# One pass over two attention blocks and a feed-forward block: earlier stack loads, a reordered slot plan, masked maxima in one instruction, a shared last tile, and a query norm applied as a factor

## What is computed

```python
# causal attention, 16 heads of 16, the whole 2048 x 2048 triangle
dot = jnp.einsum('bqhd,bkhd->bhqk', q, k)
dot = jnp.where(causal[None, None], dot, -jnp.inf)
attn = jax.nn.softmax(dot, axis=-1)
out = jnp.einsum('bhqk,bkhd->bqhd', attn, v)
...
# one layer of the fourth block: windows of 128 tokens, 8 heads of 64, then the gated feed-forward
q = l2norm(q) * qs
k = l2norm(k) * ksc
q, k = rotary_xpos(q, k)
o = local_attention(q, k, v)          # each window sees itself and the one before
x = x + o @ wo
h = (h - mu) / jnp.sqrt(var + 1e-05) * lg + lb
h = h @ w1 + b1                       # w1 is 256 x 1364
a, g = jnp.split(h, 2, axis=-1)       # 682 columns each
h = a * jax.nn.gelu(g, approximate=False)
x = x + h @ w2 + b2
```

## Time and profile before

| | us |
|---|---|
| three runs, median (lowest to highest) | 4441.09 (4441.04 to 4442.19) |
| the profiled execution, its own time | 4444.75 |
| its span, first to last instruction | 4443.1 |
| PE busy | 3852.1 (87%) |
| DVE busy | 2924.3 (66%) |
| ACT busy | 2046.0 (46%) |
| POOL busy | 894.0 (20%) |

### The profile page before, as it was taken

How to read it: one execution, slowest core, us unless ns; L and a number is a source line. 1 busy time by engine, 2 the same in 40 slices (tenths; PEclk the granted TensorE clock), 3 DMA queues, 4 the chain that set the end, 5 groups by cost and what they waited for, 6 DMA issues and landing times. The chain is left out here.

```text
span 4443.1 us, 60919 instructions
## 1 busy us (share of the span) xinstructions
PE 3852.1 (87%) x20308; PEld 1852.5 (42%) x20308; DVE 2924.3 (66%) x6609; ACT 2046.0 (46%) x3685; POOL 894.0 (20%) x800
## 2 busy tenths in 40 slices
PE   7898977898978989898969899579899699888989
PEld 6233334233334545454533333343333355454545
DVE  3987766887756652665349787659787566436643
ACT  2365642365645541455124566324566455315541
POOL 1101013101023321332230010150010333223322
PEclk8799988799989999999988999888999899999999
DMA  3212002212010010000031110021110100100000
GB/s 79 40 18 40 3 2 48 32 16 41 4 58 8 1 48 6 21 6 6 19 68 30 30 30 1 2 50 30 30 30 1 60 6 1 49 25 6 1 10 24
DMA packets 127249, 108.94 MB, mean 25 GB/s; under 512 B 38568, under 2 KB 120016, under 8 KB 125904
## 3 DMA queue, kind: packets, MB, share of 16 engines
q1 hardware_dynamic: 126928, 104.92, 11.6%
HBM read 41.15 MB, written 4.19 MB: 10 GB/s over the span
## 5 line engine op out<-in xcount | busy, mean ns | idle before, releaser
L751 DVE TENSOR_REDUCE chunk_max<-banks 128x1 f32<-128x512 f32 (+3 forms) x2240 | 1396.2, 669 | 188.9 <-PE banks L645 123.0
L718 ACT ACTIVATE probs<-banks 128x1024 f32<-128x1024 f32 (+3 forms) x1280 | 1083.0, 895 | 833.5 <-PE banks L686 829.6
L642 PE MATMUL banks<-stack_k,stack_q 96*128 96x512 bf16 (+3 forms) x2560 | 846.8, 377 | 137.2 <-DMA stack_k<-parts 55.0
L686 PE MATMUL banks<-stack_q,stack_k 99*128 99x512 bf16 (+3 forms) x2560 | 662.5, 350 | 11.3 <-ACT probs L718 11.3
L663 PE MATMUL banks<-probs,values_group 128*17 128x512 f32 (+3 forms) x5120 | 594.6, 536 | 16.7 <-ACT probs L718 13.9
L642 PEld LDWEIGHTS banks<-stack_k,stack_q 96*128 96x128 bf16 x2560 | 251.0, 100 | 803.5 <-DVE chunk_max L751 524.4
L609 POOL TENSOR_SCALAR_AFFINE_SELECT probs<-probs 128x512 f32<-128x512 f32 x256 | 162.9, 636 | 1749.2 <-ACT probs L718 1746.6
L1311 ACT ACTIVATE probs_l<-probs_l,nmax 128x256 f32<-128x256 f32 x512 | 255.8, 500 | 455.8 <-DVE nmax L1428 455.8
L1208 PE MATMUL banks<-k_blocks,qT 128*128 128x512 f32 x512 | 293.4, 656 | 109.4 <-issue 104.0
L1188 PE MATMUL banks<-wqkv,hT 128*128 128x512 f32 x768 | 368.2, 618 | 2.4 <-issue 2.4
L1596 PE MATMUL banks<-hnT,w 128*128 128x512 f32 x768 | 342.0, 606 | 3.5 <-ACT hnT L1619 3.5
(11 more groups left out here) (183 smaller groups left out, 4767.4 us busy)
## 6 DMA issues: line engine op xcount, KB each, us to landing
stack_q<-parts SPq DMA_DIRECT2D x384, 64.0 KB, 2.4
stack_k<-parts SPq DMA_DIRECT2D x384, 64.0 KB, 2.4
xpos<-in_c_xpos SPq DMA_DIRECT2D x4, 2048.0 KB, 8.3
wqkv<-in_L_ffn_wqkv SPq DMA_DIRECT2D x12, 512.0 KB, 11.7
w<-in_L_ffn_w SPq DMA_DIRECT2D x16, 341.0 KB, 4.0
x_tok<-in_L_attn_x SPq DMA_DIRECT2D x8, 512.0 KB, 5.9
rope<-in_c_rope SPq DMA_DIRECT2D x2, 2048.0 KB, 7.7
hs_f<-x_mid SPq DMA_DIRECT2D x16, 256.0 KB
```

The lines of the kernel that those rows point to most:

```text
L642: ins = pe.matmul(out, sq[0:KS, c, j0 + j, i * P:(i + 1) * P], sk[0:KS, cc, j0 + j, 0:width], start=True, stop=not diag, skip_group_check= ...
L686: ins = pe.matmul(ps[:, SCORE + j, off:CH], keys, sq[0:KS + PARTS, c, j, off:CH], start=True, stop=True, skip_group_check=True)
L718: act.activation(probs[:, s % 2, 2 * half:2 * half + 2, off:CH], ps[:, SCORE + 2 * half:SCORE + 2 * half + 2, off:CH], ACT.Exp)\
L751: dve.tensor_reduce(chunk_max[:, n % 2, j:j + heads, i, cc], bank[:, 0:heads * width].rearrange("p (h n) -> p h n", h=heads), AX.X, ALU.ma ...
```

## The change

In `attend`: group 2's stacks are loaded behind item 4 and group 1's behind item 0, all 48 DMAs at once; group 3's in halves behind items 9 and 10; SP waits for the last score of the group whose stacks are overwritten instead of outputs read. The values are read where they lie, without the four copies. A slot with one head on the diagonal has no mask matmul: DVE adds a wide mask (zeros, then the triangle) and takes the maximum in one instruction, built at the stage's start by a memset and a cast. RATE is 1.1. In `local_attention` keys are projected, squared and rotated first; the query is not multiplied by its norm, which instead scales the scores in the mask-and-maximum instruction, as a pointer per partition; the transposes of the next window stand ahead of the output product. In `feed_forward` the 42 last columns of both halves share one tile.

```diff
-RATE = 1.0
+RATE = 1.1
...
+MASKED = [m for m, (n, what) in enumerate(SLOTS) if len(what) == 4 and what[1] == 1 and what[3] == ITEMS[n][1]]
...
-                    turn = n % NCH - (g > 0)
-                    if g + 1 < NG and 0 <= turn < 2:
+                    items = (0,) if g % 2 or not g else (1, 2)
+                    if g + 1 < NG and n % NCH in items:
                         if g:
-                            sp.wait_ge(S["bank_read"], SLOTS.index((NCH * g - 1, "outputs")) + 1)
-                        for j in range(GH // 2):
-                            load_stack(sp, parts, stacks[(g + 1) % 2], g + 1, turn * GH // 2 + j, S[f"stack{g + 1}"])
+                            earlier = [s for s, step in enumerate(STEPS) if step[1] == g - 1]
+                            sp.wait_ge(S["scores_kq"], 2 * (earlier[-1] + 1))
+                        share = GH // len(items)
+                        first = items.index(n % NCH) * share
+                        for j in range(first, first + share):
+                            load_stack(sp, parts, stacks[(g + 1) % 2], g + 1, j, S[f"stack{g + 1}"])
...
-                                        start=True, stop=not diag, skip_group_check=True)
-                        if diag:
+                                        start=True, stop=not (diag and heads > 1), skip_group_check=True)
+                        if diag and heads > 1:
...
-                        ins = pe.matmul(ps[32 * j:32 * j + VW, PV, off:CH], vcur[:, g % 2, kt, j, :],
+                        ins = pe.matmul(ps[32 * j:32 * j + VW, PV, off:CH], values[:, kt, g * GH + j, :],
...
-                def values_of(g):
-                    if g >= 2:
-                        dve.wait_ge(S["pv_done"], len(STEPS) // NG * (g - 1) + 2)
-                    dve.tensor_copy(vcur[:, g % 2, :, :, :], values[:, :, g * GH:(g + 1) * GH, :])\
-                        .then_inc(S["values_in"], 1)
+                dve.memset(wide_mask[:, 0:CH - P], 0.0).then_inc(S["mask_in"], 1)
+                dve.tensor_copy(wide_mask[:, CH - P:CH], k["mask_qk"][:, :]).then_inc(S["mask_in"], 1)
+                dve.wait_ge(S["mask_in"], 2)
 
...
-                    dve.tensor_reduce(chunk_max[:, n % 2, j:j + heads, i, cc],
-                                      bank[:, 0:heads * width].rearrange("p (h n) -> p h n", h=heads), AX.X,
-                                      ALU.max).then_inc(S["bank_read"], 1)
+                    if m in MASKED:
+                        at = MASKED.index(m)
+                        if at >= 2:
+                            dve.wait_ge(S["bank_read"], MASKED[at - 2] + 1)
+                        dve.tensor_tensor_reduce(out=unread[:, at % 2, 0:width], in0=bank[:, 0:width],
+                                                 in1=wide_mask[:, CH - width:CH], scale=1.0, scalar=-3e38, op0=ALU.add,
+                                                 op1=ALU.max, accum_out=chunk_max[:, n % 2, j, i, cc:cc + 1])\
+                            .then_inc(S["bank_read"], 1)
+                    else:
+                        dve.tensor_reduce(chunk_max[:, n % 2, j:j + heads, i, cc],
+                                          bank[:, 0:heads * width].rearrange("p (h n) -> p h n", h=heads), AX.X,
+                                          ALU.max).then_inc(S["bank_read"], 1)
...
-    PROJECTED = ((0, 1), (), (2,), ())
+    PROJECTED = ((1, 0), (), (2,), ())
...
-                    for src, bank, ready, done in ((qn, BQ, "qn", "q_T"), (kn, BK, "kn", "k_T")):
+                    for src, bank, ready, done in ((pc[:, 0, :], BQ, "q_sum", "q_T"), (kn, BK, "kn", "k_T")):
...
                         if p == 3:
+                            if w + 1 < NT:
+                                turn_qk(w + 1)
                             if w:
                                 out(w - 1)
-                            if w + 1 < NT:
-                                turn_qk(w + 1)
...
-                    for i, rotated in enumerate(("rot_q", "rot_k")):
-                        own = slice(i * LH, (i + 1) * LH)
-
-                        pool.wait_ge(S["clamp"], 2 * w + i + 1)
-                        pool.tensor_tensor(inv_n[:, own], ssum[:, own], mhalf[:, own], ALU.pow).then_inc(S["inv_n"], 1)
-                        pool.wait_ge(S[rotated], w + 1)
-                        pool.tensor_tensor(pc[:, i, :], pc[:, i, :], psn[:, i, :], ALU.add).then_inc(S["sumsq"], 1)
+                    q, kk = slice(0, LH), slice(LH, 2 * LH)
+
+                    pool.wait_ge(S["clamp"], 2 * w + 1)
+                    pool.wait_ge(S["kn"], w)
+                    pool.tensor_tensor(inv_k[:, :], ssum[:, kk], mhalf[:, kk], ALU.pow).then_inc(S["inv_n"], 1)
+                    pool.wait_ge(S["rot_k"], w + 1)
+                    pool.tensor_tensor(pc[:, 1, :], pc[:, 1, :], psn[:, 1, :], ALU.add).then_inc(S["k_sum"], 1)
+                    pool.wait_ge(S["rot_q"], w + 1)
+                    pool.tensor_tensor(pc[:, 0, :], pc[:, 0, :], psn[:, 0, :], ALU.add).then_inc(S["q_sum"], 1)
+                    pool.wait_ge(S["clamp"], 2 * w + 2)
+                    if w >= 2:
+                        pool.wait_ge(S["maxed"], NP * (w - 1))
+                    pool.tensor_tensor(inv_q[:, w % 2, :], ssum[:, q], mhalf[:, q], ALU.pow).then_inc(S["inv_n"], 1)
...
-                    for i, (dst, done) in enumerate(((qn, "qn"), (kn, "kn"))):
-                        dve.wait_ge(S["inv_n"], 2 * w + i + 1)
-                        dve.wait_ge(S["sumsq"], 2 * w + i + 1)
-                        r3 = inv_n[:, i * LH:(i + 1) * LH].rearrange("p (h o) -> p h o", o=1).to_broadcast([P, LH, LD])
-                        dve.tensor_tensor(dst[:, :].rearrange("p (h d) -> p h d", h=LH),
-                                          pc[:, i, :].rearrange("p (h d) -> p h d", h=LH), r3, ALU.mult)\
-                            .then_inc(S[done], 1)
+                    dve.wait_ge(S["inv_n"], 2 * w + 1)
+                    dve.wait_ge(S["k_sum"], w + 1)
+                    r3 = inv_k[:, :].rearrange("p (h o) -> p h o", o=1).to_broadcast([P, LH, LD])
+                    dve.tensor_tensor(kn[:, :].rearrange("p (h d) -> p h d", h=LH),
+                                      pc[:, 1, :].rearrange("p (h d) -> p h d", h=LH), r3, ALU.mult).then_inc(S["kn"], 1)
 
                 def maximum(n):
-                    w = n // NP
+                    w, p = n // NP, n % NP
+                    if p == 0:
+                        dve.wait_ge(S["inv_n"], 2 * (w + 1))
...
-                                                       in1=m, scale=1.0, scalar=3e38, op0=ALU.add, op1=ALU.min,
+                                                       in1=m, scale=inv_q[:, w % 2, 2 * p + h:2 * p + h + 1], scalar=3e38, op0=ALU.add, op1=ALU.min,
...
-                    if p == 1 and ahead:
-                        squares(w + 1, 1)
                     maximum(n)
                     if p == 1 and ahead:
-                        rotate(w + 1, 1, (0,))
+                        rotate(w + 1, 0, (0,))
                     scale(n)
+                    if p == 0 and ahead:
+                        squares(w + 1, 1)
+                        rotate(w + 1, 1)
                     if p == 1 and ahead:
-                        rotate(w + 1, 1, (1,))
-                    if p == 0 and ahead:
+                        rotate(w + 1, 0, (1,))
+                        normalise(w + 1)
+                    if p == 2 and ahead:
                         squares(w + 1, 0)
-                        rotate(w + 1, 0)
-                    if p == 2 and ahead:
-                        normalise(w + 1)
...
-                        for i, bank in enumerate((BG, BA)):
+                        both = n == NHT - 1
+                        for bank, at in ((BA, 2 * FULL),) if both else ((BG, FULL + n * P), (BA, n * P)):
                             for t in range(KT):
-                                ins = pe.matmul(ps[:, bank + n % 2, :], w1[:, t, 1 - i, n * P:(n + 1) * P], hT[:, t, :],
+                                ins = pe.matmul(ps[:, bank + n % 2, :], w1[:, t, at:at + P], hT[:, t, :],
```

61 lines of the change are left out of this document (35 added, 26 removed).

## The result

The changed kernel took 4373.39 us (median of 4 runs, 4368.95 to 4380.62) against 4441.07 us in the same series: ratio 0.9849, 95% interval 0.9832 to 0.9866. It is 68 us faster, where I had forecast 156 us, and lies outside my range. TensorE, ScalarE and GpSimd are the engines that the profile calls PE, ACT and POOL.

| stages | before, us each | after, us each | sum of four | forecast |
|---|---|---|---|---|
| attend | 490.54, 490.37, 490.19, 490.38 | 470.56, 470.18, 471.02, 470.22 | -79.5 | -85 |
| local attention | 318.99, 318.48, 318.85, 318.46 | 328.12, 321.48, 328.14, 322.27 | +25.2 | -48 |
| feed-forward | 144.23, 152.90, 144.23, 149.39 | 141.32, 145.00, 141.33, 143.34 | -19.8 | -23 |

What follows compares the result with a forecast made beforehand. PE was taken to bound attend's steps and the feed-forward, a chain through DVE and ACT local attention. Terms of 85 + 48 + 23 = 156 us gave 4285 us, 3.5% faster; range 4240 to 4348.

Steps and rivals of the forecast that it cites:

- The stall: Attend, step 58: PE waits for a key-stack load; earlier loads were to gain 16.0 us an attend.
- 4.2 + 0.3: Attend's lead-in: seven slots fewer save 4.2 us; dropping the first values copy at the start gains 0.3 us.
- the lower end: Attend: DVE's fused mask-and-maximum on 512 columns costs no more than the maximum alone, 0.60 us; upper end 0.84.
- -0.8 by my terms: Each attend: moved slots +1.5 us, masks -6.5 us, new plan's steps without or with six slots +4.2 us.
- Rivals 3 to 6: In attend: cast beside memset 4260 us, 8%; stall stays 4349, 3%; DVE bounds steps 4345, 4%; slower clock 4509, 2%.
- the sum of -0.68 us a window: Local attention: shortening of the DVE and ACT chain that sets the window, 10.2 us over 15 windows.
- three terms: Local attention's chain: pair 1's maximum 0.88 us earlier, `kn` multiplication before pair 2's +0.60, pair 3's maximum -0.40.
- PE keeps 1.05 us of idle: Local attention: moved transposes do not help by themselves, since ACT reaches its copies only after pair 3's exp.
- rival 6: Attend's steps: PE falls to 1.2 GHz, making the kernel slower than before, 4509 us at 20 such steps; 2%.
- PE becomes the bound: Local attention: the chain shortens by all the idle, 26 us a stage instead of 10.2, 4222 us; 6%.
- `kn` meets POOL: Local attention: `kn` waits up to 1.27 us on the chain for POOL's query addition, windows longer, 4361 us; 7%.
- the 1.7 that I had: Feed-forward: two matmuls fewer per chunk at 0.865 us each, 1.73 us a chunk.

Runs made afterwards that it cites:

- the run: The changed kernel with the key-stack loads issued where the kernel before issued them: 4436.71 us, ratio 0.9986; the placing is worth 17.3 us an attend.

## Why the prediction was right and wrong

**Attend, -85: right.** The stall was 18.83 - 3.11 = 15.7 us by the two exps and 17.3 by the run. The lead-in with the start, from attend's first instruction to ScalarE's first exp, went from 52.57 to 48.40 us, -4.2 where I had 4.2 + 0.3. DVE's first maximum comes 7.03 us after the stage's start where it came after 7.43, since the cast ended with the memset as I had said. For the fused maximum I chose the lower end, 0.60; it takes 0.69 us with the next one 0.61 behind, which is the plain maximum's own rate. The rest (masks, moved slots and plan), -0.8 by my terms, is 0.0 to +1.6 by difference. Rivals 3 to 6 did not occur.

**Local attention, -48: wrong by 73 us, of the 82 by which the three kinds of stage fell short.** The step that failed is the sum of -0.68 us a window. Its three terms were right in kind: without the pointer they make 0.59, and one by one, in the maxima's starts of that run's window against the kernel before, -0.85, +0.61 and -0.36 us where I had -0.88, +0.60 and -0.40. The clamp is never held again (170 to 173 ns in all 128), and `kn` is not held by GpSimd in the windows. What the sum lacked is a term of its own: the operand that the change puts into the eight maxima, +0.36 us a window, which left 0.23. I had looked for the cost of the instructions that the edit moves, and taken the one that it only re-parametrises for the same instruction.

The larger part is the second step: "PE keeps 1.05 us of idle", with the clock taken for granted. I had weighed a fall of the clock for attend alone (rival 6), although show this stage with 1.73 us of waiting in each window, and the kernel before had windows of 19.93 us for me to see. The wait did not shrink, it grew to 1.89 us: the window lost 0.23 us, and TensorE's own busy time 0.39 (16.72 to 16.33), which I had not counted either. Falls in 24 more windows cost 41 us. The sum of the miss: falls 41, the operand 22, the smaller gain of the three terms 60 x 0.09 = 5, the remaining 5, by difference, at the stages' starts. If the operand had cost nothing, nearly both would have gone: that kernel, which leaves the queries' norm out, ran in 4299 us, 14 from the forecast. Even there the idle stretch was 1.53 us and not 1.05, and that the falls stay away is nothing that my sum had reasoned: the nearness of 4299 would have been luck in part.

**The rivals in local attention.** "PE becomes the bound" at 4222 us: not in this kernel, since ScalarE's order stood against it, as I wrote; one move there gave 4232. "`kn` meets POOL" at 4361 us came near the measured number for a wrong reason: GpSimd's addition for the query got longer instead (median 1.65 us where it was 1.27), off the chain.

**Feed-forward, -23: nearly right.** TensorE's tiles of a chunk went from 20.76 to 19.05 us, the 1.7 that I had. In the second layer's stages a chunk's pitch went from 32.79 to 31.31 us, 1.49 less: the wait for the last tile's product grew from 0.69 to 0.92 us. In chunk 1 of the first layer's stages I gave the gain as lost to DVE's normalisation; it turned into a loss, the pitch going from 32.80 to 34.47. TensorE's timeline there:

```profile
1665.94 1.09 PE L1602 MATMUL banks<-identf,hn 128*128 128x128 f32 x8 [1.96 <-DVE hn L1668]
```

The wait ahead of the transposes is 1.96 us where it was 0.25, and the granted clock is at 0.5 from 1667.6 to 1671.1, over the product with w2. It looks like what local attention does, once more, in two chunks, 3.3 us; no run tests it here.

## What to carry to other kernels

Where TensorE waits a little in each turn of a loop, look at the granted clock turn by turn before you cost anything there: here 0.25 us more of waiting cost 1.25 us a turn, and work that nobody reads was worth 60 us. Cost every instruction whose operands an edit changes, even if it only swaps a constant for a pointer. And when a chain through several engines sets a loop, the cheap move is often the order on the engine that holds the last link: ScalarE's copies ahead of its exp gave twice what the change itself gave.
